# Output projection as three float32r products, rotation sums moved to GpSimd, cosine products written in place

## What is computed

```python
xn = (x - mu) * rsqrt(var + EPS) * gamma
q = (xn @ Wq)                      # 16 heads of 128
k, v = split(xn @ Wkv)             # one key and value head for all
q = q * cos + rotate_half(q) * sin
k = k * cos + rotate_half(k) * sin
attn = softmax(causal(q k^T * scale))
out = (attn @ v) as 2048 columns
return out @ Wo                    # 2048 x 256, the output projection
```

## Time and profile of the kernel before

| | |
|---|---|
| median of three runs | 1405.72 us |
| time of the profiled execution | 1405.16 us |
| its span | 1403.3 us |
| TensorE busy | 1383.5 us (99%) |
| VectorE busy | 975.1 us (69%) |
| ScalarE busy | 716.2 us (51%) |
| GpSimd busy | 437.1 us (31%) |
| granted TensorE clock, mean of the core | 0.999 |
| block A's end, block B's first matmul | 362 us |

### The profile page before, as it was taken

One profiled execution on the slowest core, in us unless ns is written; L12 is line 12 of the kernel. 1 busy time (PEld: TensorE's weight loads), 2 busy tenths in 40 slices (PEclk: granted clock), 3 DMA queues, 4 the chain that ended last, 5 costly groups with the idle time before them and its releaser, 6 DMA issues.

```text
span 1403.3 us, 55347 instructions
## 1 busy us (share of the span) xinstructions
PE 1383.5 (99%) x25185; PEld 1169.1 (83%) x25185; DVE 975.1 (69%) x1824; ACT 716.2 (51%) x940; POOL 437.1 (31%) x433
## 2 busy tenths in 40 slices
PE   8999999999999999999999999999999999999997
PEld 6788888876788888888888888888888888888884
DVE  5776677666246768677777768677777767676766
ACT  3545445443455555555465555555465555555450
POOL 4333233222223233323333233323323233324310
PEclk9999999999999999999999999999999999999999
DMA  9100000000211121211212121211212121211100
GB/s 255 37 1 32 1 31 1 31 1 2 68 53 49 33 76 51 60 50 47 65 32 66 33 78 50 61 50 47 65 32 65 32 79 50 61 50 47 50 4 8
DMA packets 38923, 66.78 MB, mean 48 GB/s; under 512 B 3717, under 2 KB 36930, under 8 KB 38690
## 3 DMA queue, kind: packets, MB, share of 16 engines
q1 hardware_dynamic: 38690, 63.24, 15.7%
HBM read 61.40 MB, written 1.84 MB: 45 GB/s over the span
## 4 chain that ended last, share of the span: by engine, by line
PE 72%; DVE 2%; issue 0%; POOL 0%; DVEq 0%
PE proj_ps L1366 20%; PE proj_ps L1357 20%; PE score_ps L1384 14%; PE sum_ps L1409 13%; PE side_ps L1444 2%; PE side_ps L1458 1%; PE side_ps L1426 1%; PE side_ps L1451 1%; DVE amax L1245 0%; DVE hidden L1267 0%; DVE sig L1277 0%; DVE hidden L1278 0%; PE side_ps L1433 0%; DVE exps L1167 0%; DVE totals L1189 0%
## 5 line engine op out<-in xcount | busy, mean ns | idle before, releaser
L1119 ACT ACTIVATE exps<-score_ps 125x1792 f32<-125x1792 f32 x192 | 320.4, 1669 | 431.1 <-PE score_ps L1384 431.1
L1167 DVE TENSOR_SCALAR exps<-exps,top 125x896 f32<-125x896 f32 x384 | 288.1, 792 | 22.1 <-ACT exps L1119 17.5
L1384 PE MATMUL score_ps<-spread,keys 32*125 32x112 f32 x6144 | 219.0, 279 | 0.0
L1158 DVE COPY vals<-proj_ps 125x512 f32<-125x512 f32 x192 | 129.5, 688 | 116.6 <-PE proj_ps L1366 114.3
L1409 PEld LDWEIGHTS sum_ps<-exps,vals 125*32 125x32 f32 x12288 | 162.4, 110 | 46.9 <-issue 34.0
L1384 PEld LDWEIGHTS score_ps<-spread,keys 32*125 32x125 f32 x6144 | 184.8, 183 | 15.4 <-issue 0.3
L1409 PE MATMUL sum_ps<-exps,vals 125*32 125x56 f32 x12288 | 190.9, 214 | 0.0
L1049 POOL TENSOR_TENSOR low<-raw_early,high 128x500 fp32r<-128x500 f32 x64 | 84.5, 1322 | 216.8 <-PE proj_ps L1357 215.9
L1111 ACT ACTIVATE keys<-proj_ps,b_k 128x500 f32<-128x500 f32 x192 | 129.9, 677 | 23.7 <-PE proj_ps L1357 20.3
L1049 POOL TENSOR_TENSOR low_early<-raw_early,high_early 128x500 fp32r<-128x500 f32 x62 | 89.4, 1459 | 168.8 <-PE proj_ps L1357 168.8
L293 POOL TENSOR_TENSOR swapped<-swapped,sin 128x448 f32<-128x448 f32 (+1 forms) x72 | 86.0, 1198 | 126.5 <-ACT swapped L530 125.5
(11 more groups left out here) (169 smaller groups left out, 2415.2 us busy)
## 6 DMA issues: line engine op xcount, KB each, us to landing
raw_early<-in_ctxT SPq DMA_DIRECT2D x64, 500.0 KB, 4.1
raw<-in_ctxT SPq DMA_DIRECT2D x32, 500.0 KB, 3.6
w_q<-in_attn_Wq SPq DMA_DIRECT2D x4, 512.0 KB, 8.6
w_o<-in_attn_Wo SPq DMA_DIRECT2D x1, 2048.0 KB, 21.7
out<-y_out SPq DMA_DIRECT2D x16, 112.0 KB, 2.7
rows<-in_x SPq DMA_DIRECT2D x1, 1344.0 KB, 17.4
raw_early<-in_ffn_gate_wT SPq DMA_DIRECT2D x1, 1024.0 KB, 9.4
raw_early<-in_ffn_val_wT SPq DMA_DIRECT2D x1, 1024.0 KB, 5.1
```

Source lines behind the costliest of these rows:

```text
L1119: nc.scalar.activation(exps[t % 2][:, :, :, :].rearrange("p h r n -> p r h n"), score_ps[0:TILE, :, 0:2 * QW].rearrange("p r (h n) -> p r ...
L1158: nc.vector.tensor_copy(vals[r][:, 2 * q:2 * q + 2, :, 0:HD], proj_ps[q][0:TILE, :].rearrange("p (k h d) -> p k h d", k=2, d=HD))\
L1167: nc.vector.tensor_scalar(tile, tile, LIMIT_LO, top[:, n, at:at + 1], ALU.max, ALU.min)\
L1384: ins = nc.tensor.matmul(score_ps[0:TILE, r, to:to + HE * S], keys[c % 2][32 * r:32 * r + 32, k, (at + half) * TILE:(at + half + 1) * TILE ...
```

## The change

The output projection's two operands are split into a high and a low float32r part, and the product is made as high x high, high x low and low x high, 48 instructions of 256 columns. The weights are split once, in step 0 (ScalarE rounds, VectorE subtracts), from raw copies that lie in buffers not yet in use. The attention output is split in each step: ScalarE's `out_half` writes the high part, VectorE's new `out_low` the low one, and it is this that now lets the next value product start. In the steps, GpSimd makes the rotation sums (`rotated`); before step 0 VectorE still does. The cosine products are written to their place in `qT` and `keyT`, and `by_cos` goes. To make room, some weights and biases of block B are loaded at its start, and its first weights and the mask share `w_q`'s place and are loaded after the last query unit.

```diff
+        O_PARTS = ((0, 8), (8, 14), (14, 16))
+
+        def out_part(w, n):
+            return w[:, O_PARTS[n][0]:O_PARTS[n][1], :].rearrange("p h n -> p (h n)")
+
+        def out_raw(n):
+            if n == 2:
+                return gate_q[:, 0, :].bitcast(F32)
+            return queries[:, :, :].rearrange("p c n -> p (c n)")[:, D * O_PARTS[n][0]:D * O_PARTS[n][1]]
...
+            for n, (first, last) in enumerate(O_PARTS):
+                sp.dma_start(out_raw(n).rearrange("p (h n) -> p h n", n=D),
+                             dram["attn_Wo"].rearrange("(h p) n -> p h n", p=P)[:, first:last, :]).then_inc(wo_in, 16)
...
             sp.wait_ge(raw_used, 3)
-            for c in range(2):
-                sp.dma_start(early.ring(c), context_chunk(dram, c)).then_inc(early_ctx_in[c], 16)
+            sp.dma_start(early.ring(0), context_chunk(dram, 0)).then_inc(early_ctx_in[0], 16)
+            sp.wait_ge(unit_filled, UNIT[("q", GROUPS - 1, AU - 1)] + 1)
+            for k, name in enumerate(("xattn_WkT", "xattn_WvT")):
+                sp.dma_start(early.w_f[:, k, :, :], dram[name].rearrange("(c p) n -> p c n", p=P)).then_inc(early_w_in, 16)
+            sp.dma_start(early.mask_i, dram["mask"]).then_inc(early_in, 16)
+            sp.dma_start(early.ring(1), context_chunk(dram, 1)).then_inc(early_ctx_in[1], 16)
...
+            def rotated(name):
+
+                r, g = ROT[name], name[1]
+                pool.wait_ge(sin_ready, r + 1)
+                pool.wait_ge(cos_ready, r + 1)
+                if name[0] == "kv":
+                    dst = keyT[g % 2][:, :, :].rearrange("p b s -> p (b s)")
+                    nc.gpsimd.tensor_tensor(dst, dst, swapped[r % 4][:, 0:GR], ALU.add).then_inc(turned_ready, 1)
+                else:
+                    dst = qT[g % 2][:, name[2], :, :, 0:S].rearrange("p b h s -> p h b s")
+                    nc.gpsimd.tensor_tensor(dst, dst, swapped[r % 4][:, :].rearrange("p (h b s) -> p h b s", h=2, s=S),
+                                            ALU.add).then_inc(turned_ready, 1)
...
                 for name in more[0:2]:
                     sines(name)
+                for name in more[0:2]:
+                    rotated(name)
...
                 for name in more[2:4]:
                     sines(name)
+                    rotated(name)
                 if j and g + 2 < GROUPS:
                     sines(("kv", g + 2))
+                    rotated(("kv", g + 2))
...
             def cosines(name):
...
                     dve.wait_ge(swap_ready, r + 1)
-                if r >= 2:
-                    dve.wait_ge(rot_ready, r - 1)
-                chain.inc(nc.vector.tensor_tensor(by_row(by_cos[r % 2][:, 0:w]), by_row(bank(name)[:, 0:w]),
-                                                  cos[:, :].unsqueeze(1).to_broadcast([P, n, S]), ALU.mult))
-                chain.wait()
+                    nc.vector.tensor_tensor(qT[g % 2][:, name[2], :, :, 0:S].rearrange("p b h s -> p h b s"),
+                                            bank(name)[:, 0:2 * GR].rearrange("p (h b s) -> p h b s", h=2, s=S),
+                                            cos[:, :].unsqueeze(1).unsqueeze(1).to_broadcast([P, 2, GROUP, S]),
+                                            ALU.mult).then_inc(cos_ready, 1)
+                dve.wait_ge(cos_ready, r + 1)
                 nc.vector.sem_inc(free(name), 1)
 
             def rotated(name):
...
+            def out_low(p, k, b):
+
+                dve.wait_ge(outT_high, 2 * (2 * p + k) + b + 1)
+                nc.vector.tensor_tensor(outT_l[:, AU * k:AU * (k + 1), b * S:(b + 1) * S],
+                                        out_ps[:, b, 0:AU * S].rearrange("p (h s) -> p h s", s=S),
+                                        outT_h[:, AU * k:AU * (k + 1), b * S:(b + 1) * S].bitcast(F32),
+                                        ALU.subtract).then_inc(outT_ready, 1)
+
+            def out_weights(n):
+
+                dve.wait_ge(wo_high, n + 1)
+                nc.vector.tensor_tensor(out_part(w_ol, n), out_raw(n), out_part(w_oh, n).bitcast(F32), ALU.subtract)\
+                  .then_inc(wo_low, 1)
...
                 less_max(p)
                 for name in more[0:1]:
-                    rotary(name)
+                    cosines(name)
                 normalise(p)
                 for name in more[1:2]:
-                    rotary(name)
+                    cosines(name)
...
                 for name in more[2:3]:
-                    rotary(name)
+                    cosines(name)
                 if p:
                     norm2_rows(p - 1)
+                out_low(p, 0, 0)
+                out_low(p, 0, 1)
                 for name in more[3:4]:
-                    rotary(name)
+                    cosines(name)
+                out_low(p, 1, 0)
+                out_low(p, 1, 1)
+                if p == 0:
+                    for n in range(len(O_PARTS)):
+                        out_weights(n)
                 if j and g + 2 < GROUPS:
-                    rotary(("kv", g + 2))
+                    cosines(("kv", g + 2))
...
+            def out_weights(n):
+
+                act.wait_ge(wo_in, 16 * len(O_PARTS))
+                nc.scalar.copy(out_part(w_oh, n), out_raw(n)).then_inc(wo_high, 1)
...
+                if p == 0:
+                    for n in range(len(O_PARTS)):
+                        out_weights(n)
                 probs_out(p, 0)
                 for name in more[2:3]:
                     swap(name)
                 out_half(p, 0, 0)
+                out_half(p, 0, 1)
                 probs_out(p, 1)
-                out_half(p, 0, 1)
...
-                pe.wait_ge(wo_in, 16)
+                pe.wait_ge(wo_low, len(O_PARTS))
                 pe.wait_ge(outT_ready, 4 * (p + 1))
                 for h in range(AH):
-                    ins = nc.tensor.matmul(to[0:ROWS, 0:D], outT[:, h, :], w_o[:, h, :], start=(h == 0),
-                                           stop=(h == AH - 1))
+                    for n, (x, w) in enumerate(((outT_h, w_oh), (outT_h, w_ol), (outT_l, w_oh))):
+                        ins = nc.tensor.matmul(to[0:ROWS, 0:D], x[:, h, :], w[:, h, :], start=(h == 0 and n == 0),
+                                               stop=(h == AH - 1 and n == 2))
...
             load(2, 0, 2)
+            late = ((w_xo[:, :, :], dram["xattn_WoT"].rearrange("(a p) n -> p a n", p=P)),
+                    (ln_gamma[:, :], dram["xattn_gamma"].partition_broadcast(ROWS)),
+                    (ln_beta[:, :], dram["xattn_beta"].partition_broadcast(ROWS)),
+                    (gate_b[:, :], dram["ffn_gate_b"].partition_broadcast(ROWS)),
+                    (val_b[:, :], dram["ffn_val_b"].partition_broadcast(ROWS)),
+                    (out_b[:, :], dram["ffn_out_b"].partition_broadcast(ROWS)))
+            assert len(late) == N_LATE
+            for to, of in late:
+                sp.dma_start(to, of).then_inc(late_in, 16)
```

More of the change, by code:

```diff
@@ L47 @@
 TOTALS = (2, 6, 10)
-N_EARLY = 14
+N_EARLY = 8
+N_LATE = 6
 WEIGHTS_AT = 13
@@ L114, in block_a @@
         w_q = sb("w_q", [P, DC, AH * DH])
+        early.share(w_q[:, :, :].rearrange("p c n -> p (c n)"))
         w_kv = sb("w_kv", [P, DC, 2 * DH])
-        w_o = sb("w_o", [P, AH, D])
+        w_oh = sb("w_oh", [P, AH, D], F32R)
+        w_ol = sb("w_ol", [P, AH, D], F32R)
         w_xq = sb("w_xq", [P, DC, D])
@@ L141, in block_a @@
         swapped = [sb(f"swapped{n}", [P, 2 * GR]) for n in range(4)]
-        by_cos = [sb(f"by_cos{n}", [P, 2 * GR]) for n in range(2)]
         keyT = [sb(f"keyT{n}", [P, GROUP, S]) for n in range(2)]
@@ L262, in _ @@
                 if n == 0:
-                    for k, name in enumerate(("xattn_WkT", "xattn_WvT")):
-                        sp.dma_start(early.w_f[:, k, :, :], dram[name].rearrange("(c p) n -> p c n", p=P))\
-                          .then_inc(early_w_in, 16)
-                    sp.wait_ge(early_zero, 2)
+                    sp.wait_ge(early_zero, 1)
                     for to, of in early.loads(dram):
@@ L924, in block_b @@
         w_h, w_l, b_k, spread, top = early.w_h, early.w_l, early.b_k, early.spread, early.top
-        head_of, ident_h, b_v, w_xo, b_xo, res, part = (early.head_of, early.ident_h, early.b_v, early.w_xo,
-                                                              early.b_xo, early.res, early.part)
-        ln_gamma, ln_beta, gate_b, val_b, out_b = early.ln_gamma, early.ln_beta, early.gate_b, early.val_b, early.out_b
+        head_of, ident_h, b_v, b_xo, res, part = early.head_of, early.ident_h, early.b_v, early.b_xo, early.res, early.part
+        w_xo = sb("w_xo", [P, HG // 2, D])
+        ln_gamma = sb("ln_gamma", [ROWS, D])
+        ln_beta = sb("ln_beta", [ROWS, D])
+        gate_b = sb("gate_b", [ROWS, HID])
+        val_b = sb("val_b", [ROWS, HID])
+        out_b = sb("out_b", [ROWS, D])
         keys = [sb(f"keys{n}", [P, DC, CHUNK]) for n in range(2)]
```

71 lines of the change are left out of this document (35 added, 36 removed).

## The result

| | before | after |
|---|---|---|
| median of 15 runs each | 1405.14 us | 1408.43 us |
| lowest and highest | 1402.73, 1407.08 | 1407.39, 1411.56 |
| span of the profiled execution | 1403.3 us | 1407.8 us |
| TensorE busy | 1383.5 us | 1367.4 us |
| VectorE busy | 975.1 us | 1002.4 us |

The ratio after to before is 1.0028, its 95% interval 1.002 to 1.0036: 3.3 us slower, the forecast was 3.9 on the profiled execution. TensorE has 16.1 us less work and the kernel is not faster: all of the saving, and a little more, has become waiting.

A forecast was written before the change was run, and what follows sets the result against it. TensorE was taken as the bound, busy 245.7 of 246.6 us in steps 2 to 13. Head +6.0, steps 2 to 13 -2.3, step 14 -0.4, step 15 +0.6 gave +3.9 on 1405.2: forecast 1409 us, range 1396 to 1421.

The forecast's parts named there:

- Part 1: Output projection: 48 products at 118 ns take 5.64 us instead of 6.98, gaining 1.34 a step, 21.4 in all.
- Parts 2 and 5: Before the second value product: low half's chain stalls TensorE 0.8 us, 1.45 or 1.75 in quantising steps; net -2.3.
- Part 3: In the steps, norm2_rows, all in SBUF, waits for one GpSimd operation: 0.8 us instead of 0.41.
- the gap: GpSimd's new sum waits for its own sine product to finish; that pause lets VectorE in after one operation.
- Part 4: Rotation sums on GpSimd: nothing gained or lost; L418 may be held 1.1 us, leaving 1.2 of room.
- Part 6: Weight split in step 0: VectorE's 4.5 us precede less_max(1), first projection starts 5.7 later; head +6.0 us.
- Part 7: Last two steps: step 14 -0.4 us; in step 15 the subtractions queue behind held norm2_rows, +0.6.
- Part 8: In-place cosines, loads moved to block B's start, early loads put off: 0 us; up to 5 if a context chunk is late.
- A: In the steps, VectorE reaches norm2_rows before GpSimd, stalls 0.35 us, the gain arrives: -8.1, 1397 us; chance 0.23.
- B: VectorE starves through GpSimd's sine product and sum, 1.1 us more in 13 steps, +14: 1423 us; chance 0.16.
- C: Weight split hidden in step 0, less_max(1) not delayed: -4.3 us, 1405; chance 0.10.
- D: Projection products run at 218 ns like float32, +3.5 us a step, +56: 1465; chance 0.05 together with late loads.

The follow-up runs named there:

- experiment 3: Kernel before with rotation sums on GpSimd, in-place cosines and moved loads only, float32 projection kept: 1404.29 us, ratio 0.9994.
- experiment 4: Changed kernel with GpSimd's sum of unit 1 put behind the sine product of unit 2, so GpSimd has work queued: 1433.34 us, ratio 1.0197.
- experiment 2: Changed kernel with the rotation sums of all steps back on VectorE: 1427.21 us, ratio 1.0155 to the kernel before.
- experiment 5: Changed kernel without VectorE's weight subtraction, low weights zero, all 48 products kept: 1403.41 us, ratio 0.9989 to the kernel before.
- experiment 6: Changed kernel with 26 spare matmuls filling TensorE's hole ahead of the first projection: 1408.12 us, ratio 1.0028 to the kernel before.
- experiment 1: Changed kernel with VectorE's norm2_rows moved behind the low-half subtractions: 1398.44 us, ratio 0.9948 to the kernel before.
- experiment 8: Changed kernel with norm2_rows behind the subtractions, first projection in float32, weight split in pieces over steps 0 and 1: 1393.4 us, ratio 0.9919.

## Why the prediction was right

**Part 1, the projection.** Forecast 5.64, measured 5.69 to 5.73 in steps 2 to 13. The saving over these twelve steps was 15.0 us and not 16.1: 0.8 of the difference is the new projection's 0.05 to 0.09 over the 5.64, the rest that the projection before took 6.91 in five of the steps and not 6.98. The stretch from the scores to the projection became 0.9 us shorter in all, which I didn't forecast. In the even steps 2 to 12 it is shorter by the same 0.10 in experiment 3, so that part (0.6) isn't the projection's; its cause stays open.

**Parts 2 and 5, the stalls.** Forecast 0.8 plain and 1.45 or 1.75 in the quantising steps. Measured, over the 3.06 of before: 0.70 in steps 4, 12 and 13, 0.9 in 8, 1.0 in 2, 6 and 10, 1.19 in 5 and 9, 1.07 in 11, 1.33 and 1.37 in 3 and 7. Sum 12.2, forecast 13.8. The chain was right in its order and its releaser; steps 2, 6 and 10, which I counted as plain, have VectorE's scaling of a weight (L503, 1.29) ahead of `residual` and are a kind of their own. -15.0 + 12.2 - 0.9 = -3.7 against -3.8 measured.

**Part 3, the block.** One operation at a time in the steps, as said: L487 took 412, 868 and 3520 ns (smallest, median, largest), the largest in step 15, the 3.52 of before. The reason I gave, the gap, is only half of it (experiment 4). L441, with one operand in PSUM, took between 606 and 626 ns in all 64 cases, whatever GpSimd did. The Trainium skill, "SBUF — State Buffer", section "Who interferes with whom", says that a VectorE instruction with at most one SBUF input, outside the 2-port modes, doesn't contend with GpSimd. The trace agrees with it for L441.

**Part 4, the sums.** Nothing gained or lost: experiment 3. L471 (the old L418) is held for one more operation, 1827 ns at the median where it is 1091 undisturbed, and in step 6 it ends at 169.88, 2.3 ahead of the turning. I had left it 1.2 of room: it starts 0.6 earlier behind the scores than before (7.97 us against 8.60), since VectorE has a sum less to make, and I hadn't counted that here. What I missed is their worth for the rest of the change: without them the chain is 0.5 to 1.2 longer in every step (experiment 2). I had costed the edits one by one, and this one has no price of its own.

**Part 6, the head: the term that was mis-sized.** +8.6 instead of +6.0. ScalarE's split ahead of scores(1) costs 1.2 where 1.4 was forecast. Three terms differ by more. The first projection starts at 61.53 and not 60.3 (+1.2), 0.3 of it from a later start (52.01) and the rest because VectorE's split takes 5.5 us (52.01 to 57.52) and not 4.5; its last piece, beside a GpSimd sine product, took 1.61 for 512 columns, where the 4.5 allows 0.7: the same hold as everywhere. I had applied it to the steps but not here. The projection takes 7.94 and not 5.64 (+2.3): the clock, at its lower level behind a hole of 5.6 us. I had worked out a hole of that size and not asked what TensorE does after standing. The stall in step 1 is 0.7 and not 1.7 (-1.0), because the slow projection gives VectorE time to finish; experiments 5 and 6 show it at 1.5 once the projection is prompt. 6.0 + 1.2 + 2.3 - 1.0 = 8.5.

**Part 7, the last steps.** Step 14 -0.65 against -0.4. Step 15: the second value product comes 5.37 behind the first where it came 2.75, but the first comes 0.7 earlier, so from scores(15) it is 1.9 late, where 2.0 was forecast. The last projection starts 19.2 us after scores(15) against 17.7 before, 1.5 later and not 1.9, since the turning of the norm (at 347.44 before) stood 0.3 longer behind the value product then, waiting for `norm2_rows`; less 1.2 for the projection: +0.3.

**Part 8.** Experiment 3 bears it out as a whole. The late loads landed in 3.9 to 7.5 us, and no engine waited for one.

So the total came out near in part by luck, because its errors cancel: the head was 2.6 too low, the steps 1.5, step 14 0.25 and step 15 0.3 too high. The mechanisms of the waits were right; the clock was missing. **The rivals:** A wanted `norm2_rows` ahead of GpSimd; that didn't happen by itself, but experiment 1 takes it off the path and lands at 1398.4, next to A's 1397. B exists (experiment 4), at 1433 where I gave it 1423: a starved step costs 5.5 us and not 1.1, in four steps and not thirteen, and what sets it off is not what I wrote. C is out: VectorE's subtraction delays `less_max`, by more than I said. D is out by the 0.12 between starts; its price was too low as well, since the 1409 to which I added 56 us already contains the gain of 21.4 that D takes away.

## What to carry to other kernels
Moving work off an engine that isn't the bound can be worth nothing or some 18 us; ask what will hang behind that engine's queue once the rest of the change is in. If a new operation must release the bounding engine, look at what stands ahead of it in the same queue and can go behind: one moved call turned +3 us into -6. And when a sum contains a hole in TensorE of some microseconds, price the clock after it as well, and check every such hole, not only the largest: filling one showed the drop at the next.

## What the runs showed of the hardware
- TensorE's granted clock fell to 0.50 (1.2 GHz) behind 5.6 us of standing and stayed there for 4.9 us of full work; float32r products then start 0.21 us apart instead of 0.12. Behind 2.9 us of standing it fell in one kernel (experiment 6) and not in another (after) at the same place of the program, and behind 2.46 us it fell in step 7 and not in step 3 of one and the same execution (experiment 2). Behind a wait of 2.0 us it was 0.61 in the window 58 to 62 (experiment 8; the projection had started at 56.46). What decides it is open; the runs show only that short holes aren't safe.
- A VectorE instruction with all its operands in SBUF waited for one GpSimd operation, or through a run of them: four in experiment 4 (4.29 us), GpSimd's split and spread in step 15 (3.52). Where GpSimd paused, if only for 0.08 us between two dependent operations, VectorE got in every time. Where it didn't, `norm2_rows` of experiment 4 got in if the operation under way had itself begun after a pause, and waited on if that one had followed another directly, with the exception of step 8. The cause isn't shown: the two groups differ in the moment of its arrival too.
- The hold goes both ways: two GpSimd sums in a row took 3.16 us (168.89, step 6 of after) while VectorE's L471 was on until 169.88; two in a row took 2.21 at 206.81 in experiment 4.
